# Feed-forward set-up of a decoder layer: covariance from centred rows, and variance, scaled keys and first similarities in halves

## What is computed

```python
# x: (16, 100, 128) after the second layer norm (x2 in the kernel)
q = jnp.einsum('bnd,de->bne', x, w_q)            # w_q: 128 x 2048
mean = jnp.mean(q, axis=(0, 1))
var = jnp.var(q, axis=(0, 1))
q = (q - mean) * jax.lax.rsqrt(var + BN_EPS) * bn_gamma + bn_beta
q = q.reshape(b, n, 2, H, KD).transpose(2, 0, 1, 3, 4)    # H = 8, KD = 128
sim = jnp.einsum('pbnhd,hkpd->pbnhk', q, keys)            # 32 keys for each of 2 x 8
sx, ix = jax.lax.top_k(sim[0], TOPK)
sy, iy = jax.lax.top_k(sim[1], TOPK)
...                                   # best 8 of the 64 sums, then the experts:
h = jnp.einsum('bnd,bnhkd->bnhk', x, wd)
h = jax.nn.softmax(scores, axis=-1) * gelu_new(h)
out = jnp.einsum('bnhk,bnhkd->bnd', h, wu)
```

## Time and profile before

| | us |
|---|---|
| median of 3 runs | 1365.36 |
| lowest of these | 1363.19 |
| time of the profiled execution | 1367.09 |
| its span (first to last instruction) | 1365.3 |
| `ffn`'s first instruction in the profile | 1052.31 |
| first search for the best (L1383) starts | 1098.72 |
| first `oneh` (L1471) starts | 1120.50 |

### The profile page before, as it was taken

One profiled execution on the slowest core, in us unless ns is written; L12 is line 12 of the kernel. 1 busy time (PEld: TensorE's weight loads), 2 busy tenths in 40 slices (PEclk: granted clock), 3 DMA queues, 4 the chain that ended last, 5 costly groups with the idle time before them and its releaser, 6 DMA issues. The chain is left out here.

```text
span 1365.3 us, 32623 instructions
## 1 busy us (share of the span) xinstructions
PE 1152.9 (84%) x12753; PEld 905.5 (66%) x12758; DVE 1154.6 (85%) x2860; ACT 871.6 (64%) x1202; POOL 621.0 (45%) x512
## 2 busy tenths in 40 slices
PE   3567899999999999999999999999996548777778
PEld 2464677677776777767676776777775527776668
DVE  5886898998999899998999989988886278999984
ACT  0347778888888888887888788888874532122121
POOL 2354667565765657657576675657230000000000
PEclk9768899999999999999999999999998665676656
DMA  7017999999999999999999999999997200000000
GB/s 153 1 29 134 182 175 187 199 192 193 187 190 192 194 192 190 195 190 175 201 193 189 192 185 196 178 181 166 191 184 147 56 0 2 5 5 5 5 5 6
DMA packets 671122, 185.78 MB, mean 136 GB/s; under 512 B 655829, under 2 KB 668537, under 8 KB 670841
## 3 DMA queue, kind: packets, MB, share of 16 engines
q1 hardware_dynamic: 670968, 183.71, 79.3%
HBM read 19.51 MB, written 0.82 MB: 15 GB/s over the span
## 5 line engine op out<-in xcount | busy, mean ns | idle before, releaser
L1042 PE MATMUL ps<-pT,xa_hi 128*128 128x128 f16 x2288 | 386.4, 219 | 60.4 <-ACT uT L874 60.4
L851 ACT ACTIVATE e<-ps,bias 128x1444 f32<-128x1444 f32 (+1 forms) x208 | 305.5, 1469 | 171.8 <-DVE bias L923 171.4
L921 DVE TENSOR_REDUCE nmax<-ps 128x1 f32<-128x1444 f32 (+1 forms) x208 | 344.5, 1656 | 51.0 <-PE ps L1026 50.1
L1046 PE MATMUL ps<-pT,xa_hi 128*128 128x128 f16 x2288 | 386.6, 219 | 0.9 <-DMA pT<-p 0.9
L1043 PE MATMUL ps<-pT,xa_lo 128*128 128x128 f16 x2288 | 386.6, 219 | 0.0
L933 DVE TENSOR_TENSOR p<-e,p 128x1408 f16<-128x1408 f32 (+3 forms) x288 | 299.5, 1081 | 11.4 <-ACT p L859 8.5
L859 ACT ACTIVATE p<-e 128x1408 f16<-128x1408 f32 (+1 forms) x208 | 289.6, 1392 | 7.6
L1042 PEld LDWEIGHTS ps<-pT,xa_hi 128*128 128x128 f16 x2288 | 224.0, 99 | 91.7 <-issue 78.8
L811 POOL TENSOR_TENSOR p<-e,p 128x1408 f16<-128x1408 f32 (+1 forms) x128 | 196.6, 1557 | 183.7 <-ACT p L859 183.7
L1024 PE MATMUL ps<-xT_hi,q_hi 128*128 128x512 f16 (+1 forms) x624 | 229.5, 368 | 8.4 <-DMA xT_lo<-xa_lo 7.2
L1043 PEld LDWEIGHTS ps<-pT,xa_lo 128*128 128x128 f16 x2288 | 224.0, 99 | 12.2
(11 more groups left out here) (225 smaller groups left out, 1913.6 us busy)
## 6 DMA issues: line engine op xcount, KB each, us to landing
raw<-in_ctx SPq DMA_DIRECT2D x16, 704.0 KB
pT<-p SPq DMA_TRANSPOSE x416, 4.2
f_wq<-in_L_ffn_w_q SPq DMA_DIRECT2D x1, 1024.0 KB, 5.0
f_wqt<-in_ffn_wq_t SPq DMA_DIRECT2D x2, 512.0 KB, 7.1
raw<-in_ctx SPq DMA_DIRECT2D x48, 18.0 KB
x_tok<-in_x SPq DMA_DIRECT2D x1, 800.0 KB
out_x<-ost SPq DMA_DIRECT2D x6, 128.0 KB, 2.0
wk_t<-in_wk_t SPq DMA_DIRECT2D x1, 512.0 KB, 5.7
```

The source lines that it names most:

```text
L851: act.activation(e32[t % E_BUF][rows, :], score_banks(t)[rows, 0:T], ACT.Exp, bias=bias[rows, t % N_BUF:t % N_BUF + 1]).then_inc(e_done, 1)
L921: dve.tensor_reduce(nmax[rows, k:k + 1], score_banks(t)[rows, 0:T], AX_X, ALU.max, negate=True).then_inc(max_done, 1)
L1042: pe.matmul(out, hi, ph, start=n == 0, stop=False)
L1046: pe.matmul(out, hi, pl, start=False, stop=False)
```

## The change

It touches `cross` in one place and the set-up of `ffn` throughout.

- **Sum of tokens.** In `cross`, POOL adds each finished batch of x2 to `x2sum`, 15 times (slot 7 of a batch's 13 tiles). In `ffn` DVE adds the last batch (`total`), and PE makes the column mean from it, once spread over all rows and once as a column.
- **Covariance from centred rows.** DVE subtracts the mean from x2 as it lies (`xc`, four groups), and PE sums the 16 products from that. The 16 transposes back (L1512) and their copies are gone. Only the first group of four batches is turned before the covariance; the other three come after the first similarities, and DVE centres them between the first step's search and its cast of indices.
- **Loads.** `f_wq` first, then beta, gamma, keys, then the two halves of `f_wqt`, then the experts' tables; each use waits for its own semaphore.
- **Halves.** Variance, `vrs`, `kscaled`, `sim_w`, first similarities and the first search go in two halves of eight key sets. The constant (`simc_...`) comes after the variance.
- **Tables.** POOL writes `iota_c`, `iota_j` and half of `iota_w` (two quarters, one ahead of its first `vrs`, one behind its first `comb`), ACT the other half.

```diff
+                if i == 7 and 0 < b < B:
+                    pool.wait_ge(y_norm, 4 * b)
+                    pool.wait_ge(x2sum_done, b)
+                    pool.tensor_tensor(out=m["x2sum"][:, :], in0=m["x2sum"][:, :], in1=x2[:, b - 1, :], op=ALU.add).then_inc(x2sum_done, 1)
...
+            sp.dma_start(f_wq[:, :], a["L0_ffn_w_q"]).then_inc(wq_ld, 16)
+            sp.dma_start(f_bet[:, :], a["L0_ffn_bn_beta"]).then_inc(keys_ld, 16)
+            sp.dma_start(f_gam[:, :], a["L0_ffn_bn_gamma"]).then_inc(keys_ld, 16)
+            sp.dma_start(f_keys[:, :, :], a["ffn_keys_t"].rearrange("e s h k -> e (s h) k")).then_inc(keys_ld, 16)
...
+            wide_rows(0)
+            for p in range(2):
+                pool.wait_ge(var_done, p + 1)
+                pool.tensor_tensor(out=vrs[:, key_half(p)], in0=var[:, key_half(p)], in1=nhalf[:, 0:FH], op=ALU.pow).then_inc(vrs_done, 1)
...
             for i in range(NSTEP):
                 combine(i)
+                if i == 0:
+                    wide_rows(1)
...
+            for p in range(2):
+                act.wait_ge(simw_ps, p + 1)
+                act.activation(sim_w[:, sim_half(p)], ps[:, 4 + p, 0:HALF_SIM], ACT.Copy).then_inc(simw_done, 1)
+                first_out(p)
+            for k in range(1, NG):
+                turned_out(k)
...
+            dve.tensor_tensor(out=total[:, :], in0=x2sum[:, :], in1=x2[:, B - 1, :], op=ALU.add).then_inc(total_done, 1)
+            dve.wait_ge(mean_ps, 1)
+            for k in range(NG):
+                ks = slice(k * G, (k + 1) * G)
+                dve.scalar_tensor_tensor(out=xc[:, ks, :], in0=ps[0:S, 3, 0:D].rearrange("s (a d) -> s a d", a=1).to_broadcast([S, G, D]),
+                                         scalar=-1.0 / NT, in1=x2[:, ks, :], op0=ALU.mult, op1=ALU.add).then_inc(xc_done, 1)
...
+            sim_weights(0)
             pe.wait_ge(simc_done, 1)
-            pe.wait_ge(simw_done, 1)
+            pe.wait_ge(xcT_done, 1)
+            first_sims(0)
+            sim_weights(1)
+            first_sims(1)
+            for k in range(1, NG):
+                turn(k)
+            pe.wait_ge(expert_ld, 32)
+            pe.wait_ge(first_done, 2)
```

More of the change, by code:

```diff
@@ L1216, in _, with turned_out @@
         def _(act):
-            for k in range(NG):
+            def turned_out(k):
                 act.wait_ge(x2T_ps, k + 1)
-                act.activation(x2T[:, k * G * S:(k + 1) * G * S], ps[:, k, 0:G * S], ACT.Copy,
-                               accum_out=msum[:, k:k + 1]).then_inc(x2T_done, 1)
+                act.activation(x2T[:, group(k)], ps[:, 7, 0:G * S], ACT.Copy).then_inc(x2T_done, 1)
+            turned_out(0)
+            act.wait_ge(cov_ps, 1)
+            act.activation(cov[:, :], ps[:, 0, 0:D], ACT.Copy, scale=1.0 / NT).then_inc(cov_done, 1)
             act.wait_ge(fc_done, 6)
+            act.activation(iota_w[:, P // 2:P, :], iota_f[:, P // 2:P].rearrange("p (e a) -> p e a", a=1).to_broadcast([P, P // 2, P]),
+                           ACT.Copy).then_inc(wide_act, 1)
             act.wait_ge(simc_ps, 1)
             act.activation(sim_c[0:1, :], ps[0:1, 6, :], ACT.Copy).then_inc(simc_hi, 1)
[L1224 to L1233, removed]
             act.wait_ge(simc_rest, 4)
@@ new lines, in centred, with weighted_cov @@
+            def centred(k):
+                dve.wait_ge(x2T_done, k + 1)
+                dve.tensor_scalar(xcT[:, group(k)], x2T[:, group(k)], mean[:, 0:1], None, ALU.subtract).then_inc(xcT_done, 1)
+            def weighted_cov(k):
+                ns = slice(4 * k, 4 * k + 4)
+                dve.wait_ge(cw_ps, k + 1)
+                if k == 0:
+                    dve.wait_ge(wqt_ld, 32)
+                dve.tensor_tensor(out=cw[:, ns, :], in0=ps[:, k, :].rearrange("e (n d) -> e n d", n=4),
+                                  in1=f_wqt[:, ns, :], op=ALU.mult).then_inc(cw_done, 1)
@@ new lines, in variance, with safe_variance, scaled_keys @@
+            def variance(k):
+                ns = slice(4 * k, 4 * k + 4)
+                dve.wait_ge(cw_done, k + 1)
+                dve.tensor_reduce(var[:, ns], cw[:, ns, :], AX_X, ALU.add).then_inc(sum_done, 1)
+            def safe_variance(p):
+                dve.wait_ge(sum_done, 2 * p + 2)
+                dve.tensor_scalar(var[:, key_half(p)], var[:, key_half(p)], 0.0, EPS, ALU.max, ALU.add).then_inc(var_done, 1)
+            def scaled_keys(p):
+                ns = key_half(p)
+                dve.wait_ge(vrs_done, p + 1)
+                dve.wait_ge(keys_ld, 48)
+                dve.tensor_tensor(out=gain[:, ns], in0=vrs[:, ns], in1=f_gam[:, ns], op=ALU.mult).then_inc(gain_done, 1)
+                dve.wait_ge(gain_done, p + 1)
+                dve.tensor_tensor(out=kscaled[:, ns, :], in0=f_keys[:, ns, :],
+                                  in1=gain[:, ns].rearrange("e (n a) -> e n a", a=1).to_broadcast([KD, FH, KEYS]), op=ALU.mult).then_inc(kscaled_done, 1)
@@ L1307, in _ @@
+            centred(0)
+            for k in range(2):
+                weighted_cov(k)
+                variance(k)
+            safe_variance(0)
+            weighted_cov(2)
+            variance(2)
+            weighted_cov(3)
+            scaled_keys(0)
+            variance(3)
+            safe_variance(1)
             dve.wait_ge(simc_hi, 1)
@@ L1314, in _ @@
             dve.tensor_copy(c_part[:, 1, :], c_rest[:, 1, :]).then_inc(simc_rest, 1)
[L1316 to L1333, removed]
+            scaled_keys(1)
             def weigh(i, n):
@@ L1399, in step @@
                     norm_shift(i - 2)
+                if i == 0:
+                    for k in range(1, NG):
+                        centred(k)
+                    dve.wait_ge(narrow_done, 1)
                 dve.wait_ge(top_done, 2 * i + 2)
```

158 lines of the change are left out of this document (90 added, 68 removed).

## The result

The changed kernel takes 1347.89 us (median of four runs, 1344.79 to 1350.26) against 1364.62 before, a ratio of 0.9871 with a 95% interval of 0.9854 to 0.9889: 1.3% faster, by the medians 16.7 us. One of the four runs before took 2264.54; the ratio leaves it out as a slow one. Beside the experiments it was timed again, with 1348.01 and a ratio of 0.9881 (0.9855 to 0.9906). Its profiled execution took 1347.50, with a span of 1345.8. The forecast was 1349.

A forecast was written before the change was run, and what follows sets the result against it. The set-up was taken as a serial chain through the engines, 49.6 us to the second search, with PE between half and full clock. 13.3 + 4.3 - 1.1 = 16.5 off the median 1365.4 gave 1349, range 1342 to 1356.

The forecast's parts named there:

- Covariance: Set-up of `ffn`: covariance waits only for the mean, copied at 1061.0 instead of 1074.26; 13.3 won, bounds 12.3 and 14.2.
- First block to second search: Set-up, from DVE's first weighted block to the second search: 22.1 in halves instead of 26.4; 4.3 won.
- S: Moment when DVE starts the first weighted block in the set-up, forecast at 1062.2.
- ACT's table: Set-up: ACT's half of `iota_w`, 6.9 from 1061.0, ends ahead of the constant's turn; free, 0.3 to spare.
- Given back: First step: three centrings of 0.36 each between DVE's search and its cast of the indices; 1.1 lost.
- Loads: Set-up: `f_wq` lands ahead of need, `f_wqt` just in time; cost 0, upper bound 2.6 lost.
- Later steps: The six steps after the first keep their lists; clock phases may shift the end some 2 us either way.
- Clock up in the second half: Rival, set-up: PE stays at 1.00 through similarities and second key products; 4.1 more won, 1345; chance 0.22.
- Additions onto the path: Rival, cross-attention: POOL's 15 additions, 0.35 each, come onto the path, 5.3 in all, 1354; chance 0.10.
- Slow casts: Rival, set-up: POOL's table casts at 9 ns a column delay the first `vrs`; 44.5 lost, 1393; chance 0.03.

The follow-up runs named there:

- The version for the rest of the chain: Changed kernel with no table on ACT, DVE's last sum and first centring behind the constant, ACT's third constant row behind half of `sim_w`: ratio 0.9852, median 1344.79.
- the version with one wait: Changed kernel with PE waiting for all eight loads ahead of the weights' products: ratio 0.9917, median 1354.48 us.

## Why the prediction was right

The sum was made of three terms, and all three can be read off.

*Covariance, 13.3 forecast.* Its copy ended at 1074.26 - 1052.31 = 21.95 after the start before and 1061.86 - 1052.76 = 9.10 now: 12.85, within the bounds of 12.3 and 14.2. I had put the clock's rise between 5.3 and "never"; it came 7.5 after PE's start, and in none of the ten profiles before 6.6, and 32 passes took 6.6 where 6.2 had been taken as the middle.

*First block to second search, 4.3 forecast.* 26.4 before and 21.3 now, 5.1. The two similarities (2.4 each and not 2.6) and the key products (3.3, not 3.5) were each a little cheaper. That the constant's operations come onto the chain was right; they started at S + 6.3 and not S + 6.6. ACT's table, put down as free with 0.3 to spare, was on the path by 0.1. The version for the rest of the chain shows that this place cost some 1.1 to 1.4.

*Given back, 1.1 forecast.* From the second search to the first `oneh` it was 1120.50 - 1101.94 = 18.56 before and 1104.06 - 1084.41 = 19.65 now, 1.1 more. The three centrings took 1.30, and the first of them was held by POOL's second quarter, which ended at 1089.98:

```profile
1089.57 1.30 DVE L1347 TENSOR_SCALAR xcT<-x2T,mean 128x400 f32<-128x400 f32 x3
1086.38 3.60 POOL L1217 CAST iota_w<-iota_f 128x4096 f16<-128x4096 f32 x1
```

ACT wasn't late: from the cast of the indices to `oneh` it is 13.27 in both kernels.

Together 12.85 + 5.13 - 1.09 = 16.9, where 13.3 + 4.3 - 1.1 gave 16.5. The mechanism is the one forecast, term by term. That the sum came within 0.4 is in part luck: the covariance gave 0.4 less and the stretch to the search 0.8 more.

*Loads, 0 forecast.* Right, and by little: where the covariance came 0.4 earlier after the start, DVE waited 0.2 for `f_wqt`. The bound of 2.6, for `f_wqt` landing with the last byte, wasn't put to the test: the version with one wait holds PE's products back and not DVE's first block, and costs 5.9.

*Later steps, "some 2 either way".* From the first `oneh` to the end of the span it was 244.8 before and 241.7 after, 3.1 less; this was named and a little undersized. By the table and the two windows it is the clock's phase. It makes up the rest of the 19.5 by which the spans differ, since the changed kernel's feed-forward part began 0.45 later, and it belongs to this one execution: the medians differ by 16.7 to 17.8.

*Rivals.* "Clock up in the second half" didn't happen: PE restarted at 1073.5 and stayed at 0.50 until 1088. Of the reasons against it the row of 12.1 at half clock held. The other, PE's wait for the constant, isn't borne out: the clock fell within the first 0.5 of that wait, and was just as low where the wait was cut to 1.13. "Additions onto the path" was tested with four times as many and fell. "Slow casts" fell: 0.88 ns a column and not 1.5 or 9. The row of 128 columns misled, since its fixed part had been put too low at 0.1: by the casts of 2048 and 4096 columns it is some 0.2. The Trainium skill, "GPSIMD Engine Reference", section 3.1, gives 1.03 cycles per element at 1.2 GHz for an operation with at most two ALU steps, as an estimate 0.86 ns, and the trace agrees.

One thing the prediction didn't see, and was lucky about: POOL's casts stop some DVE operations. It had read the 3.51 of the earlier trace rows as work that goes on while POOL subtracts, where the ends show a hold, and it asked what this does to the additions and not what it does to the tables. The centring took 3.40 instead of 0.43. It was hidden with 2.9 to spare, DVE's wait for the first weighted block. The rule of the Trainium skill that it cited for the additions, "GPSIMD Engine Reference", section 8, names DVE instructions in a two-port mode as well as those with two SBUF inputs. The trace agrees for the subtractions, which have two SBUF inputs; the centring has one SBUF tile and a scalar column, and whether it ran in such a mode no run here shows.

## What to carry to other kernels

Before costing a removed stage, look at what its first instruction waits for. Here one semaphore for eight loads was worth 9.3 by itself and the rest of the change 11.0 without it, but together they gave 16.9. A wait that PE sits out costs twice, once for itself and once for the half clock afterwards: 4.8 and 1.0 of the 5.9 measured. And when work is moved to POOL to free another engine, list the DVE operations that run beside it. Here a `tensor_scalar` from SBUF to SBUF and a subtraction of two SBUF tiles were held until POOL's operation ended, whatever their own length; a sum over an SBUF tile wasn't.

## What was not expected of the hardware

- A running POOL cast holds certain DVE operations until it ends: a `tensor_scalar` over 400 fp32 columns took 3.40 instead of 0.43, and one over 8 columns 1.56 instead of 0.17. Of three casts in a row it waits for the running one only. In the same places products with one PSUM input (0.69) and sums over an SBUF tile (0.69) kept their times. In the cross-attention DVE's subtractions of two SBUF tiles wait in the same way, 14 times.
- POOL's cast with a broadcast input runs at 0.88 to 0.92 ns a column (3.60 for 4096, 1.89 for 2048).
- The clock doesn't rise at a fixed place of the work: over the same first products of the feed-forward part it rose 6.6 to 7.6 after PE's start. Kernels with equal instructions differ by up to 2.9 over four steps, and the windows above show the rise ahead of a step's last product in one and behind it in the other.
- The clock can fall soon after PE stops: within 0.5 of its last product, behind 1.97 of products at full clock and an idle stretch of 1.76 ahead of those.
- The issue of a load can stand 3.4 to 3.8 in SyncE's queue while earlier loads are under way (`f_keys` before, `f_down` with one wait). Which one stands depends on the order; with the new order it was `f_down` in every profile, for 2.4 to 3.75.
